# Sixteen key-block differences per quad instead of twelve in a three-engine attention loop, with a new order table

## The reference, cut to what matters

```
xn = layernorm(x)                              # x: 4 x 2048 x 256
q, k, v = low-rank projections of xn           # 16 heads of 16
scores = where(causal, q @ k^T / 4, -inf)      # per head 2048 x 2048
y = softmax(scores) @ v
out = x + y @ Wc + ffn(xn)                     # ternary feed-forward of width 1024
```

## Time and profile before

| | |
|---|---|
| median of 3 runs | 2087.46 us (2086.99 to 2091.14) |
| profiled execution, its own time | 2089.05 us |
| its span | 2087.3 us |
| attention loop, first to last copy of `Y` | 616.3 to 1959.7 us |
| one quad in the steady part | 84.3 to 84.9 us |
| last quad | 75.6 us |

### The profile page before, as it was taken

How to read it: one execution, slowest core, us unless ns; L and a number is a source line. 1 busy time by engine, 2 the same in 40 slices (tenths; PEclk the granted TensorE clock), 3 DMA queues, 4 the chain that set the end, 5 groups by cost and what they waited for, 6 DMA issues and landing times. The chain is left out here.

```text
span 2087.3 us, 42600 instructions
## 1 busy us (share of the span) xinstructions
PE 1944.2 (93%) x14289; PEld 735.4 (35%) x14289; DVE 1796.7 (86%) x4744; ACT 1583.0 (76%) x2078; POOL 359.0 (17%) x618
## 2 busy tenths in 40 slices
PE   7799999999789999999999999999999999999698
PEld 6454555555322222222222222222222222222165
DVE  5688888888889999999999989899999999997187
ACT  2466656655349999999999989999999999999500
POOL 0111111111121221212212112121221221212000
PEclk8999999999769999999999999999999999999789
DMA  4123322334340302303213032030330312300376
GB/s 162 41 86 90 95 77 86 94 96 101 86 72 2 53 11 43 53 2 52 36 19 53 2 53 43 12 53 2 53 53 2 52 20 35 53 2 13 99 212 198
DMA packets 146213, 123.32 MB, mean 59 GB/s; under 512 B 82068, under 2 KB 132668, under 8 KB 144572
## 3 DMA queue, kind: packets, MB, share of 16 engines
q1 hardware_dynamic: 137324, 112.55, 24.7%
q10 hardware_dynamic: 8720, 8.65, 1.3%
HBM read 69.50 MB, written 50.86 MB: 58 GB/s over the span
## 5 line engine op out<-in xcount | busy, mean ns | idle before, releaser
L1043 ACT ACTIVATE prob<-st 128x1024 f32<-128x1024 f32 (+3 forms) x1280 | 1072.0, 898 | 84.5 <-PE st L1162 75.7
L1175 PE MATMUL pv<-prob,V 128*32 128x512 f32 (+3 forms) x5120 | 599.2, 543 | 0.1
L1138 PE MATMUL sm<-K,Q 48*128 48x512 f16 (+3 forms) x2176 | 543.0, 351 | 17.2 <-DVE pm L1101 5.1
L1086 DVE CUSTOM_DVE_ANT_0 sm<-sm,mask 128x128 f32<-128x128 f32 (+3 forms) x1024 | 490.5, 510 | 61.0 <-PE sm L1138 53.7
L1101 DVE TENSOR_REDUCE pm<-sm 128x1 f32<-128x512 f32 x768 | 494.7, 684 | 15.6 <-PE sm L1138 13.1
L1162 PE MATMUL st<-Q,K 50*128 50x512 f16 (+3 forms) x2560 | 473.9, 353 | 21.4 <-ACT prob L1043 11.1
L1001 POOL TENSOR_SCALAR_AFFINE_SELECT prob<-prob 128x256 f32<-128x256 f32 x512 | 206.0, 409 | 1118.7 <-ACT prob L1043 1113.6
L1138 PEld LDWEIGHTS sm<-K,Q 48*128 48x128 f16 x2176 | 173.9, 94 | 391.6 <-DVE pm L1101 157.9
L1097 DVE CUSTOM_DVE_ANT_0 sm<-sm,excess 128x512 f32<-128x512 f32 x384 | 264.8, 716 | 26.9 <-PE sm L1138 18.0
L1162 PEld LDWEIGHTS st<-Q,K 50*128 50x128 f16 x2560 | 125.7, 93 | 409.8 <-ACT prob L1043 322.7
L1036 ACT ACTIVATE excess<-st 128x1024 f32<-128x1024 f32 x188 | 190.4, 1031 | 5.4 <-DVE pm L1097 0.7
(11 more groups left out here) (151 smaller groups left out, 1902.4 us busy)
## 6 DMA issues: line engine op xcount, KB each, us to landing
Q<-scratch_q SPq DMA_DIRECT2D x102, 128.0 KB, 4.0
K<-scratch_k SPq DMA_DIRECT2D x102, 128.0 KB, 6.1
x<-in_x SPq DMA_DIRECT2D x18, 512.0 KB, 4.5
scratch_v<-Vs SPq DMA_DIRECT2D x64, 128.0 KB, 2.0
scratch_r<-R SPq DMA_DIRECT2D x16, 512.0 KB, 3.2
V_raw<-scratch_v SPq DMA_DIRECT2D x16, 512.0 KB, 8.6
scratch_y<-Y SPq DMA_DIRECT2D x64, 128.0 KB
Yt<-scratch_y SPq DMA_DIRECT2D x16, 512.0 KB, 5.7
```

The costliest lines, as they stand in the source:

```text
L1043: act.activation(prob[(slot * UNITS + k) % PT][:, :, 0:width], st[number % ST][:, :, 0:width], ACT.Exp)\
L1086: dve.tensor_tensor_reduce(x, x, mask[:, CH - width:], 1.0, -3e38, ALU.add, ALU.max, pm[:, row, t, k:k + 1]).then_inc(sm_read, 1)
L1138: pe.matmul(dst[:, 0:block_width(t, k)], lhsT=Q[slot][r, h // 2, t * P:(t + 1) * P], rhs=K[slot][r, h // 2, k * CH:k * CH + block_width(t, ...
L1175: i = pe.matmul(pv[2 * DH * h:2 * DH * (h + 1), CH - width:CH], lhsT=V[slot][:, j, h, :], rhs=prob[(slot * UNITS + 2 * n + h // 2) % PT][: ...
```

## The change

The rule that says which query tiles use a difference is widened: before, group c = 3 and the first half of the heads of group c = 2; now both halves of c = 2. A quad has 131 entries instead of 139 (32 plain, 32 paired, 64 edge and 3 rows, against 48, 24, 64 and 3), and 16 differences instead of 12. `AHEAD` falls from 75 to 71, and the differences that come ahead of their quad (`XAHEAD`) rise from 4 to 7. The order string is a new one of 267 tokens instead of 271; a line of it stands here for the four.

```
-                pair = c == 3 or c == 2 and hp == 0
+                pair = c >= 2
...
-AHEAD = 75
+AHEAD = 71
...
 TIMETABLE = (
-    "ssmmwmmsmswsmmswxmmxmwsmsmmssmwmswsmsmmwxmmsmwmmsmmxmwmmssmmwmmsmsws"
+    "mmsmxwmsmmswmsmwxsmmwsmmsssmmxwsmmswmsmmwxmmmxwsmmmsmmxmsmwsmmmswsmm"
...
-    "swmmssmwsmmmswsmmswsmmmswmsmsmmwsmmsmwmsmsmmwmsmxmmsmwmmsxmmsmwsmsm"
+    "swsmsmmwsmmsmwsmmswsmmswsmmmxmmswsmmmxmmswmsmmxmwsmxmmmswsmmsss"
```

More of the change, by code:

```diff
@@ L789 @@
 TIMETABLE = (
-    "ssmmwmmsmswsmmswxmmxmwsmsmmssmwmswsmsmmwxmmsmwmmsmmxmwmmssmmwmmsmsws"
-    "mmxmxmmwmmssmmsmsssmmwmsmxmmsmwsmmwxmsmmwsmmmsmswsmmsmwsmsmmwsmmxmms"
-    "mmwsmsmmwmsmmswmsmmswsmxmmswmsmsmsmmwsmmmsmwwmmssmmwsmmmswsmmmswsmmm"
-    "swmmssmwsmmmswsmmswsmmmswmsmsmmwsmmsmwmsmsmmwmsmxmmsmwmmsxmmsmwsmsm"
+    "mmsmxwmsmmswmsmwxsmmwsmmsssmmxwsmmswmsmmwxmmmxwsmmmsmmxmsmwsmmmswsmm"
+    "swsmmxmmswsmmsssmsmmwsmmwsmxmmwmxmsmwsmmmswsmmswsmmmswsmmswmsmmsmwsm"
+    "mmswmsmmxmmxwsmmswsmsmsmssmmswmsmmmswwmxmmsmwmmsmsmwsmmmswsmmmswsmmm"
+    "swsmsmmwsmmsmwsmmswsmmswsmmmxmmswsmmmxmmswmsmmxmwsmxmmmswsmmsss"
 )
```

## The result

The changed kernel takes 2098.14 us, median of 13 runs (2088.84 to 2104.08), against 2087.95 for the kernel before in the same comparison (2085.13 to 2094.29). The ratio is 1.0043, with a 95% interval of 1.0026 to 1.0060. It is slower by about 9 us (by the ratio; the medians differ by 10), where 2081 was forecast.

A forecast was written before the change was run, and what follows sets the result against it. The bound was taken as how well PE, ACT and DVE loads match over short stretches, not one engine's total. Terms -4.5 - 0.7 - 1.5 = -6.7 us from the median 2087.46 gave 2081 us, range 2052 to 2110.

The forecast's parts named there:

- The slower rival: Steady quads: ACT's waits are PE's answer time, not DVE's doing, so +9, 2096 us (up to 2142); chance 0.29.
- The sign for the forecast: Length of a steady quad: the prediction is wrong if it lies outside 83 to 85.5 us.
- the order's term: Steady quads: the new order lets ACT's waits fall from 8.1 to 4.5 us; -0.3 us x 15 quads = -4.5.
- -0.7: Last quad: the 16-token count gives 75.3 us with the new order, 76.0 before.
- DVE's -4.6: DVE per steady quad: loses 16 plain entries, gains 8 paired; -4.6 us, to 69.0.
- ACT's +3.7: ACT per steady quad: gains four Relus of 0.92; +3.7 us, to 80.0.
- PE's +0.2: PE per steady quad: gains four differences, loses eight entries; 0 to +0.8 us, taken as +0.2.
- The prologue: Ahead of the loop: 71 entries instead of 75, three more differences; -1.5 us, between -2.2 and +0.4.
- The new waits: Shorter leads in the loop: some tenths for DVE within its slack; ACT's `excess` wait 0, at most +0.6 a quad.
- Row DMAs: Score units of c = 2 waiting for row DMAs: 5.8 us in the whole run, forecast not to grow.
- Clearly faster: Steady quads: ACT becomes sole bound, running as it does alone; quad 82.0, -37, 2050 us; chance 0.20.
- The clock: Start and quad 0: three more prologue differences bring full speed sooner, at most 4.5 us, 2077 us; chance 0.05.

The follow-up runs named there:

- third run with repeated Relus: Kernel before with four Relus a quad, at the third of every three differences, taken twice over (same result): 2145.74 us, ratio 1.0265.

## Why the prediction was wrong

**The slower rival came true in its number.** It had a quad of 85.1 and 2096 us, from ACT's listed busy time plus the 2.1 us of idle time that the second half of the last quad showed; measured were 85.6 and 2098, inside the stated range of 2052 to 2110 but on the side that had a chance of 0.29. Its reading, that DVE had little to do with ACT's waits, holds: DVE's relief alone changed nothing. Its other half, that ACT's total is then the bound, doesn't: 3 us less of ACT (busy 80.0) would by the same sum give 82.1 a quad, and it stayed at 85.6. So the rival met its number partly by luck. The sign that I gave for it, an ACT wait that stays at 4.4 us and a quad over 87, was wrong too: the wait fell to 1.5. The sign for the forecast failed by a little, a steady quad of 85.6 where 83 to 85.5 was asked.

**The step that failed is the order's term**, -0.3 us x 15 = -4.5. Measured is about +1.0 x 14 (together 14.4), which refutes the term. The last quad, where -0.7 stood, took 1.0 more, but with a dip of 3.4 us that the kernel before didn't have there; in steady quads with a single such dip it cost 1.8 us in the kernel before, 2.1 in the changed one, and from about 1.1 (third run with repeated Relus) to 2.6 (halved Relus) in the others, by which it would be -1.6 to -0.1 without (an estimate), so that part is neither confirmed nor refuted. The forecast needed ACT's waits to fall from 8.1 to 4.5 by the same count; they fell to 85.6 - 80.0 = 5.6. It came from summing each engine's prices over 16 neighbouring tokens and taking the largest. Such a sum lets an engine that is ahead at one token use that lead up to 15 tokens later. What the runs showed in its place is that such leads hardly pay: work taken from any one engine gave 0 to 20% back, work added to PE or ACT cost 70 to 85% of itself. That is what a chain looks like in which at each unit the later of two hand-overs counts. PE and ACT share two `st` tiles, so PE can be ready only one unit early; the halved Relu above shows it at one place. That it is the number of tiles and not something else in the hand-over is argued and not shown: no kernel with a third `st` tile was run, and none with PE and ACT relieved together. Two results fit the chain only loosely: the added Relus cost nearly the same at three sets of places, and more than half of the narrowed exponentials kept ACT's own pace.

That a length of 16 gave back the 84.0 and 76.0 of the kernel before was no proof of the method: I had picked the length for it, and the lengths beside it gave -0.9 to +0.4. Their spread was larger than the term, and I took them as the method's error though all share its fault.

**The parts.** DVE's -4.6 was right in size (busy 78.3 to 74.9 by the listed time, which counts tails) and worth nothing. ACT's +3.7 was right (79.3 to 83.0), and by the runs with added Relus 80 to 85% of it, about 3.1 us, would land in the quad (an estimate; no run adds just this). PE's +0.2 can't be told apart from the order in these runs; in the old order the rule as a whole cost +4.1 (88.7 against 84.6), so some 1.0 is left for PE and for entries and differences that stand in less fitting places. The new order gave 3.1 back, and +1.0 stayed. I had asked whether the order could turn a rise of 3.7 into nothing, and took a yes from a count that couldn't tell.

**The prologue**, -1.5 forecast: the start up to the end of quad 0 is 3.5 us shorter. The run with halved Relus, whose prologue has the same instructions and whose quad 0 has less work, took 695.9 us to the same point, against 689.2 for the changed kernel and 692.7 for the one before. The clock explains the difference in part. From 606 to 624 us, in the changed kernel and in that run:

```profile
606.00:624.00 18.00, 17.47 (x144) 4.78 (x142) 15.77 (x48) 17.75 (x22) 5.51 (x8) 1.00 0.03 6
```

```profile
606.00:624.00 18.00, 17.93 (x87) 4.12 (x87) 10.65 (x33) 11.18 (x14) 3.68 (x4) 0.50 0.04 7
```

The stretch at a granted clock of 0.50 that begins ahead of the loop lasts 54.6 us in the changed kernel's trace, 58.0 in the kernel before and 75.1 in that run. So the changed kernel's start also holds 3.4 us less of the slow clock. A dip of that length cost about 1.1 to 2.6 us in steady quads, so by that estimate a third to three quarters of the 3.5 is the clock's; how much of the rest is the work, single profiles don't show.

**The new waits** didn't appear. DVE waited 8.6 us for ACT at paired entries in the whole run (6.1 before), on an engine with slack, and ACT waits 0.7 us in all ahead of its Relus in the loop. Row DMAs: PE's listed weight-load wait is 7.8 us against 5.8, a little more where none was forecast. **Clearly faster** failed. Its stretch of 18 units at 0.92 each stands in the last quad of the kernel before, where PE has sums but no entries between the score units:

```profile
1940.01 1.06 PE L1175 MATMUL pv<-prob,V 128*32 128x512 f32 x8
1941.00 0.91 PE L1162 MATMUL st<-Q,K 50*128 50x512 f16 x4
1941.84 1.07 PE L1175 MATMUL pv<-prob,V 128*32 128x512 f32 x8
```

In a steady quad PE has 139 entries to fill besides, 131 after the change. **The clock**: the slow stretch at the start did end sooner, by little, as above, but no run shows that the three more differences brought this: the run with halved Relus has the same ones in its prologue, and 75.1 us of it; the dips in steady quads cost nearly the same in both profiles. The changed kernel's times lie between 2089 and 2104, those of the kernel before between 2085 and 2094 here but between 2083 and 2098 over its 25 runs beside the first experiments, so the spread tells nothing.

## What to carry to other kernels

Before trading work between engines, ask how far each can run ahead of the next. Here, with two `st` tiles between PE and ACT, relief of one engine gave at most a fifth of itself, while added work arrived to 70 to 85%, so an exchange that is even in totals (4.6 us off one, 3.7 onto another) is a loss unless the order can absorb it. Test it cheaply: take the work off alone and add the work alone, in the old order; here the two runs gave 0 and +3.6 us a quad, and so would have said, before any search for an order, how much an order has to bring back.

## What the runs showed of the hardware

Taking about 15 us of issue from PE in each quad of the changed kernel made it slower, 2150 us against 2098: the granted clock fell to 0.90 and 0.96 in the two quads shown, and over the whole run the mean was 0.879 against 0.969. So in this kernel the lighter PE work came with a lower granted clock, and the two together with a longer time; what lowered the clock, no run shows. A single dip of 3.4 us at a granted clock of 0.50 cost 1.1 us of a quad in the third run with repeated Relus (89.1 against 88.0), 1.8 in the kernel before (86.4 against 84.6), 2.1 in the changed one (87.7 against 85.6) and 2.6 in the run with halved Relus (88.2 against 85.6). The dips in steady quads of both full kernels, where PE was busy over 95% of the window by the listed time, remain unexplained here.
